# DLRM tower on one core: eight tables looked up by matmul in the first group, 260 gathers, gathered blocks taken four ahead, and half-block runs of Gram strips

## The reference, cut to what matters

```python
e = stack([tbl_f[ids[:, f]] for f in range(26)], axis=1)     # 2048 x 26 x 128
all_emb = concatenate([bottom[:, None, :], e], axis=1)       # 2048 x 27 x 128
gram = einsum('bfd,bgd->bfg', all_emb, all_emb)
z = gram[:, triu_i, triu_j]                                  # 351 pairs
h = concatenate([z, bottom], axis=1)                         # 479
h = maximum(h @ W_top1 + b_top1, 0)                          # 512
h = maximum(h @ W_top2 + b_top2, 0)                          # 256
y = h @ W_top3
```

## Time and profile before

| | us |
|---|---|
| median of 3 runs | 356.62 (356.36 to 359.17) |
| the profiled execution | 355.85 |
| its span, first to last instruction | 354.1 |
| PE busy | 329.4 (93%) |
| POOL busy (264 gathers) | 255.7 (72%) |
| DVE busy | 245.1 (69%) |
| ACT busy | 205.0 (58%) |
| granted PE clock | 1.0 throughout |

### The profile page before, as it was taken

The page is one execution under the profiler, slowest core; times in us unless marked ns, Lnnn a source line. Parts: engine busy times, 40 slices in busy tenths (PEclk is TensorE's granted clock), DMA queues, the critical chain, the costliest instruction groups (busy, mean ns, idle before and its releaser), DMA issues.

```text
span 354.1 us, 13649 instructions
## 1 busy us (share of the span) xinstructions
PE 329.4 (93%) x5840; PEld 295.9 (84%) x5840; DVE 245.1 (69%) x720; ACT 205.0 (58%) x349; POOL 255.7 (72%) x274
## 2 busy tenths in 40 slices
PE   0788989999999999999999989999999999999996
PEld 0676979998888989979888889879999798888885
DVE  1999989996676978459763987549885597431412
ACT  3684777522345659549478567565865587572222
POOL 5777777777777777777777777777777777777720
PEclk9999999999999999999999999999999999999999
DMA  6668649422228685576685496584769476532210
GB/s 206 189 173 219 184 127 316 121 55 54 55 54 159 95 165 114 83 155 136 148 115 98 98 175 123 121 99 99 158 125 141 99 130 113 115 83 56 56 31 1
DMA packets 64203, 42.88 MB, mean 121 GB/s; under 512 B 48784, under 2 KB 56464, under 8 KB 64016
## 3 DMA queue, kind: packets, MB, share of 16 engines
q1 hardware_dynamic: 55024, 24.38, 34.8%
q0 software_dynamic: 8448, 17.32, 20.8%
q10 hardware_dynamic: 672, 0.33, 0.3%
HBM read 31.24 MB, written 0.01 MB: 88 GB/s over the span
## 4 chain that ended last, share of the span: by engine, by line
PE 82%; DVE 9%; DMA 3%; ACT 2%; issue 2%; SPq 0%; ACTq 0%; DVEq 0%
PE hot_ps L498 30%; PE gram_ps L476 14%; PE h_ps L530 11%; PE xt_ps L498 9%; PE h_ps L575 8%; DVE onehot L731 5%; PE h_ps L527 4%; PE xt_ps L459 3%; DMA rows_sb<-in_rows_dram 2%; DVE tab L798 2%; PE zt_ps L512 2%; DMA ids_wide<-in_hot_ids_dram 1%; DVE h L788 1%; ACT turned L993 1%; DVE Z L739 1%
## 5 line engine op out<-in xcount | busy, mean ns | idle before, releaser
L445 POOL DMA_INDIRECT X<-in_table_dram,rows_sb x264 | 254.3, 963 | 82.8 <-issue 78.9
L731 DVE TENSOR_SCALAR onehot<-ids_wide,row_value 128x288 fp32r<-128x288 int16 (+2 forms) x575 | 183.9, 390 | 31.6 <-PE hot_ps L498 20.6
L498 PE MATMUL hot_ps<-onehot,tab 128*128 128x288 f32 (+2 forms) x948 | 144.6, 305 | 14.1 <-DVE onehot L731 13.8
L498 PEld LDWEIGHTS hot_ps<-onehot,tab 128*128 128x128 f32 x948 | 132.0, 190 | 17.7 <-issue 15.4
L706 ACT COPY XT<-turned 128x512 int16<-128x512 int16 x82 | 65.7, 885 | 8.7 <-DMA turned<-planes 8.7
L883 ACT COPY XT<-hot_ps 128x288 f32<-128x288 f32 (+2 forms) x66 | 40.1, 658 | 39.8 <-PE hot_ps L498 37.5
L476 PEld LDWEIGHTS gram_ps<-XT 128*27 128x27 f32 x4096 | 45.1, 104 | 20.9 <-issue 15.8
L476 PE MATMUL gram_ps<-XT 128*27 128x26 f32 x4096 | 56.3, 192 | 4.2 <-issue 1.2
L872 ACT COPY planes<-X 128x1024 int16<-128x1024 int16 x41 | 44.3, 1082 | 17.5 <-DMA X<-in_table_dram,rows_sb 17.5
L530 PE MATMUL h_ps<-stage_sb,w_sb 128*128 128x256 f32 (+3 forms) x192 | 44.2, 366 | 0.0
L530 PEld LDWEIGHTS h_ps<-stage_sb,w_sb 128*128 128x128 f32 (+1 forms) x192 | 35.0, 191 | 4.3
(11 more groups left out here) (54 smaller groups left out, 137.8 us busy)
## 6 DMA issues: line engine op xcount, KB each, us to landing
stage_sb<-in_hot_dram SPq DMA_DIRECT2D x20, 256.0 KB, 3.5
X<-in_table_dram,rows_sb POOLq DMA_INDIRECT x264
ids_wide<-in_hot_ids_dram SPq DMA_DIRECT2D x8, 360.0 KB, 5.3
ids_wide<-in_hot_ids_dram SPq DMA_DIRECT2D x4, 400.0 KB, 4.0
bottomT<-in_bottom_t_dram SPq DMA_DIRECT2D x8, 128.0 KB, 3.9
w_sb<-in_w_dram SPq DMA_DIRECT2D x1, 1024.0 KB, 7.0
turned<-planes SPq DMA_TRANSPOSE x41
stage_sb<-in_hot_dram SPq DMA_DIRECT2D x5, 128.0 KB, 2.9
```

The lines of the kernel that those rows point to most:

```text
L445: pool.indirect_dma_start(X[:, n % RING, k, :], None, table, bass.IndirectOffsetOnAxis(idx[:, column:column + 1], 0)).then_inc(gathered[n ...
L498: mm = pe.matmul(hot_bank(i)[:, 0:width(n)], tab[u][:, part, D * c:D * (c + 1)], onehot[p % ONEHOTS][:, c - BITES[u][h], 0:width(n)], star ...
L731: compared = dve.tensor_scalar(onehot[p % ONEHOTS][:, c - BITES[u][h], 0:width(n)], ids_wide[:, k, 0:width(n)], row_value[:, c:c + 1], Non ...
```

## The change

- Group 0 looks up 8 tables: 70 chunks, 140 products, all 256 wide. The four further tables of tiles 0 and 1 are now two, and are fetched for both tiles by one side unit of four gathers into Z, after units 0 and 1. Gathers: 264 to 260.
- The X ring has 5 slots instead of 4. ACT splits unit b+4 in its step b instead of b+2 (so 50 units go by DMA, 10 to 59, instead of 41). PE transposes unit b+4 at block b while that is below 10.
- PE works in pairs of blocks throughout. Strips come 16 to a run, each between lookups or layers; two quarters of layer 1, or both tiles of layer 2, stand together between the two runs of the pair's first block. `z_transposes` moves to a pair's end. Layer 2 writes the two tiles to two halves of its bank.
- The third bank for lookups is used from group 2 on, was 3. Ids are loaded three blocks before a group's end.
- In the head DVE clears gram_ps and adds the row offsets later, makes the one-hots of a piece before its subtraction, and the first piece is halved.
- `last_blocks` starts at block 56. Units 60 to 63 are transposed by PE inside the strips of blocks 58 to 60 and ahead of those of 62; layer 2 of tile 14 comes after the last strip.

PE at blocks 16 to 19 before: the last rows of a group 288 wide, the pair of 64 strips, z, and the next pair with layer 1 (hot_ps and xt_ps are lookup banks, gram_ps the strips).

```diff
-ALWAYS = 16
-SOMETIMES = 4
-HOT = TABLES - ALWAYS
-HOT_BASE = HOT - SOMETIMES
+GATHERED = 16
+EXTRA = 2
+HOT = TABLES - GATHERED
+HOT_BASE = HOT - EXTRA
 FOUR = 4
 BLOCKS = P // PAD
-TILE_COLUMNS = BLOCKS * (1 + ALWAYS // FOUR)
-BOTTOM_SLOT = ALWAYS + SOMETIMES
+TILE_COLUMNS = BLOCKS * GATHERED // FOUR
+BOTTOM_SLOT = GATHERED + EXTRA
-RING = 4
+RING = 5
 TURNED = 2
-AHEAD = 2
 SHARING = 2
...
-SPLIT_STEPS = 6
+SPLIT_STEPS = 3
...
-LAST = BLOCKS * (TILES - 2)
+UNITS = BLOCKS * TILES
+LAST = UNITS - 2 * BLOCKS
+THIRD = 2
-THIRD = 3
...
+LEAD = 4
+SIDE = UNITS
+STREAM = [0, 1, SIDE] + list(range(2, UNITS))
+HEAD_TURNS = {1: 0, 2: 1, 4: SIDE, 6: 2, 7: 3}
+TURN_FROM, TURN_TO = 10, UNITS - BLOCKS
+BY_DMA = list(range(TURN_FROM, TURN_TO))
+DIRECT = [n for n in STREAM if n not in BY_DMA]
 NTH = {n: k for order in (DIRECT, BY_DMA) for k, n in enumerate(order)}
+MOVED = {n: k + 1 for k, n in enumerate(STREAM)}
...
-    PIECE = [pieces(c, PIECE_MAX) for c in HC]
+    PIECE = [([0, 2] if u == 0 else [0]) + pieces(c, PIECE_MAX)[1:] for u, c in enumerate(HC)]
...
+                if b == STARTS[n + 1] - 3 and n + 2 < GROUPS:
+                    load_low_ids(n + 2)
+                if b == STARTS[n] and 0 < n < GROUPS - 1:
                     load_high_ids(n + 1)
+                if b + LEAD in BY_DMA:
+                    turn(b + LEAD)
...
+            for n in STREAM:
+                if n == BLOCKS:
                     pool.wait_ge(idx_ready, 1)
+                if n == SIDE:
+                    pool.wait_ge(side_ready, 1)
+                    for k in range(FOUR):
+                        pool.indirect_dma_start(side[:, k, :], None, table,
+                                                bass.IndirectOffsetOnAxis(side_sb[:, k:k + 1], 0)
+                                                ).then_inc(side_gathered, 16)
+                    continue
                 before = n - RING
                 if before >= 0 and before in BY_DMA:
                     pool.wait_ge(planes_ready, NTH[before] + 1)
                 elif before >= 0:
                     pool.wait_ge(xt_full, NTH[before] + 1)
...
+                dve.wait_ge(h2_full, t + 1 if t >= TILES - 2 else t + 2 - t % 2)
+                dve.tensor_tensor(h2[:], h2_half(t), vec_sb[:, 0, :], ALU.add).then_inc(h2_moved, 1)
...
+                    dve.wait_ge(side_loaded, 16)
+                    dve.tensor_tensor(side_sb[:, 0:FOUR], side_sb[:, 0:FOUR], side_sb[:, FOUR:2 * FOUR], ALU.add
+                                      ).then_inc(side_ready, 1)
+                    dve.wait_ge(rows_loaded, 16)
+                    dve.tensor_tensor(chunks[:, 1:, :], chunks[:, 1:, :],
+                                      starts.to_broadcast([P, TILES - 1, TILE_COLUMNS]), ALU.add).then_inc(idx_ready, 1)
                 for p in asked_of(q):
                     one_hot(p)
+                split_second(q)
+            dve.memset(gram_ps[:], 0.0).then_inc(pads_zero, 1)
...
-                split_words(UNITS_OF.get(b + AHEAD, []))
+                for i in placed_in(b):
+                    if i not in ended(b):
+                        place_hot(i)
                 for p in pieces_ended(b):
+                    if is_last(p) and ASKED[p][0] in placed_in(b):
+                        place_hot(ASKED[p][0])
                     one_hot_share(p + ONEHOTS)
-                for i in placed[1:]:
-                    place_hot(i)
+                split_words(b + LEAD)
                 if j == 2:
                     place_bottom(t + 1)
                 for q in LATE_PIECES[PER_STEP * b:PER_STEP * (b + 1)]:
                     split_first(q)
-                moves(b + 1)
+                if b + LEAD < TURN_FROM:
+                    move(b + LEAD)
+                if b + LEAD - 1 in BY_DMA:
+                    move(b + LEAD - 1)
...
+            def pair(b):
+
                 t, j = b // BLOCKS, b % BLOCKS
+                between = t >= 2 and (t % 2 == 1 or j == 2) and b + 2 < LAST
+                if between:
                     lookups(*slice_of(b))
+                    strips(b, 0, 1)
+                    layers(t, j)
+                    strips(b, 1, RUNS)
                 else:
                     for run in range(RUNS):
                         lookups(*slice_of(b, run, run + 1))
+                        strips(b, run, run + 1)
+                if b + LEAD < TURN_FROM:
+                    transposes(b + LEAD)
+                for run in range(RUNS):
+                    lookups(*slice_of(b + 1, run, run + 1))
+                    strips(b + 1, run, run + 1)
+                if not between:
+                    layers(t, j)
+                if j == 0 and t > 0:
+                    z_transposes(t - 1)
...
                 layer1(len(JOBS) - 2, 1)
-                gram(b + 1)
-                transposes(UNITS_OF[b + 2])
+                strips(b + 1)
                 layer1(len(JOBS) - 2, 2)
                 layer1(len(JOBS) - 2, 3)
-                gram(b + 2)
-                transposes(UNITS_OF[b + 3])
+                transposes(b + 3)
+                strips(b + 2)
+                strips(b + 3)
                 bottoms_last(0, C1 - 1)
-                gram(b + 3)
-                layer2(t - 1, 0, C1 - 1)
+                layer2(t - 1)
                 z_transpose_last(0)
```

More of the change, by code:

```diff
@@ L123, in folded_pairs, with build @@
     return out
[L126 removed]
+def build(nc, table, rows_in, side_in, hot_ids, hot_tables, bottom_t, w1, b1, w2, row_vecs, out):
     fp32, fp32r, i16, i32 = mybir.dt.float32, mybir.dt.float32r, mybir.dt.int16, mybir.dt.int32
@@ L462, in gram, with transposes @@
[L462 to L472 removed]
+            def transposes(n):
+                if n not in DIRECT:
+                    return
+                if n == SIDE:
+                    pe.wait_ge(side_gathered, 16 * FOUR)
+                else:
+                    pe.wait_ge(gathered[n % RING], 16 * FOUR * (n // RING + 1))
+                if NTH[n] > 0:
+                    pe.wait_ge(xt_moved, MOVED[DIRECT[NTH[n] - 1]])
+                for k in range(FOUR):
+                    rows = side[:, k, :] if n == SIDE else X[:, n % RING, k, :]
+                    mm = pe.transpose(xt_ps[:, P * k:P * (k + 1)], rows, ident[:])
+                mm.then_inc(xt_full, 1)
@@ L697, in move_turned, with move_direct @@
-        def move_turned(eng, copy, n):
-            t, j = UNITS[n]
-            slot = NTH[n] % TURNED
+                if u in HEAD_TURNS:
+                    transposes(HEAD_TURNS[u])
+            for b in range(0, LAST, 2):
+                pair(b)
+            last_blocks()
+        def move_direct(eng, copy, b):
+            eng.wait_ge(xt_full, NTH[b] + 1)
+            if b == SIDE:
+                copy(XT[:, 0:2 * BLOCKS, :, GATHERED:GATHERED + EXTRA],
+                     xt_ps[:].rearrange("d (k b s) -> d b s k", k=EXTRA, s=PAD)).then_inc(xt_moved, 1)
+                return
+            wait(eng, gram_full, b - KEPT + 1)
+            copy(XT[:, b % KEPT, :, 0:GATHERED].rearrange("d s (k f) -> d s k f", f=FOUR),
+                 xt_ps[:].rearrange("d (k s f) -> d s k f", s=PAD, f=FOUR)).then_inc(xt_moved, 1)
@@ L1073 @@
     out = nc.dram_tensor("out_0_dram", (P, TILES), _mybir.dt.float32, kind="ExternalOutput").ap()
-    build(nc, dram["table"], dram["rows"], dram["hot_ids"], [dram[f"hot{u}"] for u in range(HOT)],
+    build(nc, dram["table"], dram["rows"], dram["side"], dram["hot_ids"], [dram[f"hot{u}"] for u in range(HOT)],
           dram["bottom_t"], dram["w1"], dram["b1"], dram["w2"], dram["vecs"], out)
```

317 lines of the change are left out of this document (127 added, 190 removed).

## The result

The changed kernel takes 358.39 us (median of 20 runs, 357.24 to 361.89), the kernel before 356.95 on the same chips: a ratio of 1.0051, 95% interval 1.0028 to 1.0075. It is half a per cent slower, well within 1%. The forecast was 356.7, no change. The profiled execution has a span of 359.0 and took 360.73, which is 2.3 above its median: in six of the 20 runs, this one among them, the mean granted clock of TensorE is 0.995 or lower, and they take 359.4 to 361.2, while the other 14 have a median of 358.1.

A forecast was written before the change was run, and what follows sets the result against it. PE was taken as the bound, with POOL's gathers right behind. Terms of 6.6 - 2.7 - 2.9 - 2.1 + 2.0 - 1.4 + 0.6 summed to +0.1, giving 356.7 us by the median; range from just under 352.2 to 361.

The forecast's parts named there:

- Head: Before block 0: two more tables and the later gram_ps clear, less an earlier second table, add 6.6 us.
- Blocks 0 to 7: PE transposes six units instead of ten and block 4's double transposition goes: 2.7 us saved.
- the paragraph on the gathers: POOL's stream: four fewer gathers take 5.0 us off; a shift from late side-unit indices is priced at nothing.
- Blocks 8 to 15: Seven units are no longer transposed by PE: 2.9 us saved.
- Blocks 16 to 53: Sixteen strips a run, with restarts, layers and layer 2's waits, save 2.1 us; new Z waits add 2.0.
- The restart: In blocks 16 to 53, each of 43 more runs of lookups costs 0.18 us: +7.7.
- The waits for Z: PE's first strips of five even tiles (4 to 12) wait for DVE's Z: +2.0 us in all.
- The end: Last blocks and tail: units of blocks 57 to 59 leave PE, -1.4 us; later layer work adds 0.6.
- POOL's last gather: The last gather of the stream was forecast to start near 333.4 us.
- Rival 2: DVE falls behind in pairs starting an even tile, PE waits longer for Z: +5.5 us, 362.2; 12%.
- Rival 3: In the head, DVE starts the second table no sooner: +2.3 us, 359.0, no change; 10%.
- Rival 1: Restarts cost nothing or Z is never waited for; gathers bind at the last unit: -4.4 us, 352.2; 21%.

The follow-up runs named there:

- the run with one block less ahead: The changed kernel with the units PE transposes itself (4 to 9) turned three blocks ahead instead of four: 357.99 us, ratio 1.0026 to the kernel before.
- the run with 20 lookups: The changed kernel with the first block of each even tile and of tile 1 as 20 lookups, then 32 strips: 355.17 us, ratio 0.9944 to the kernel before.

## Why the prediction was right, and where it was not

It was right in the number that counts, +0.1 forecast and +1.4 measured in the medians, and in most terms. In part that was luck: a head that came 1 to 1.5 cheaper than forecast paid for some of the waits that the forecast had at nothing.

- **Head, +6.6 forecast, +6.1 measured.** PE waits 1.34 for unit 3 at its end, but block 0 could not have begun at once without that wait: it needs its one-hots too, and where PE hardly waits for unit 3 it begins at 36.59 and 37.06, which is +5.1 and +5.6. The term that was too large is the table of ten chunks. It costs DVE 3.9 (the last subtractions of the three that there are now start at 26.66, 30.56 and 34.46), not the 4.4 read from the last table before, and three times 0.5 is 1.5. The second table did start 2.3 sooner, as forecast: its first piece is begun with one-hots at 10.39 now and was begun with a subtraction at 12.69.

```profile
10.39 0.88 DVE L739 TENSOR_SCALAR onehot<-ids_wide,row_value 128x256 fp32r<-128x256 int16 x3
11.19 0.73 DVE L806 TENSOR_TENSOR tab<-stage_sb,tab 128x512 fp32r<-128x512 f32 x1
```

- **Blocks 0 to 7, -2.7 forecast, +1.9 measured.** Less 3.0 of waits and 1.45 of slow clock it is -2.5. In the two other profiles of this part it is -0.2 and -0.9, or -2.8 and -2.4 less their waits of 2.6 and 1.5. The term was sound; what failed is the paragraph on the gathers: "it has up to 5 us to spare, so I price this at nothing." The 5 us were read at the last unit, and so were the 2.9 from a gather's start to its use. Early, PE takes about 4.5 us a block and POOL 5.0 a unit, the lead of four asks for a unit earlier, and units 3, 4 and 6 were in use only 5.9, 5.0 and 6.1 after their last gather's start (31.24, 37.65 and 48.11). Four gathers fewer give 1.2. The sentence "I am wrong altogether if PE waits for XT, that is for the units four blocks ahead" named the place. The waits came, before the transpositions out of X that fill XT, and cost about a microsecond of the median rather than the forecast.
- **Blocks 8 to 15, -2.9 and -2.4**: 0.26 is a wait for Z in tile 2.
- **Blocks 16 to 53, -0.1 and -0.5.** The restart is there. In the timeline of PE of the changed kernel 18 lookups in one run last 2.54 to the next strips, nine 1.38, so a second run costs 0.22 (0.19 against the 18 that stand behind strips, 181.43 to 184.00), where 0.18 stood:

```profile
171.06 2.62 PE L516 MATMUL xt_ps<-onehot,tab 128*128 128x288 f32 x18
173.60 0.42 PE L494 MATMUL gram_ps<-XT 128*27 128x26 f32 x32
...
179.70 1.46 PE L516 MATMUL hot_ps<-onehot,tab 128*128 128x288 f32 x9
181.08 0.42 PE L494 MATMUL gram_ps<-XT 128*27 128x26 f32 x32
```

  The waits for Z in tiles 4, 6, 8, 10 and 12 are 0.56, 0.24, 0.66, 0.20 and 0.25, together 1.9 where 2.0 stood. That strips and restarts cancel could not be shown by undoing one of them, since either kernel loses 13 to 16 us without the parts around it; only the sum is shown.
- **The end, -0.8 and -0.2.** Two small waits for ScalarE and DVE, 0.56 and 0.49, took what was missing.
- **POOL's last gather** came at 336.66, 3.3 late, of which the two gathers of 2.22 in the head make 2.6. The forecast itself was sound: 333.8 to 334.2 in three of the experiments.

Rival 2 did not happen: no Z wait passes 0.7. Rival 3 did not happen either, though the time lies near its 359.0: the second table came when forecast. Rival 1 (gathers bind, faster) had the right engine and the wrong place: they hold PE up early, and once the Z waits are gone they take back in the first half what PE wins. Its other half, that a restart might cost nothing, falls with the 0.22 above: here the trace does not bear out what the Trainium skill (TensorE: Matmul & The Clock Gate, Architectural detail) would allow, loads pulled forward over the strips.

## What to carry to other kernels

Two streams that end together need not run together: read the slack of the slower one at several points of the timeline, not at the last transfer, and look for it in the waits of the engine between them (here ScalarE), since the bound engine's own waits show nothing until the slack is gone. Before a profile is explained, look at a second one of the same program: here the early part alone differed by 3 us. The lead of units, the length of a run and the orders of the helping engines are one choice: one of them changed alone lost 10 to 16 us in three trials. And six waits of 0.2 to 0.7, one line of the page, were the cheapest to repair: 3.2 us for three lines of code.

## What the runs showed of the hardware that I had not expected

A short pause of PE can be followed by a lower granted clock that costs over half as much again: after 2.52 us, and after 2.19 in the run with one block less ahead, some 1.45 us were lost on slow matmuls. After 1.89 in the run with 20 lookups the granted clock was 0.70 for 5.8 us. The length of the pause does not decide it alone: 1.77 us before unit 4, with the weights held back, left the clock at full, and so did 2.82 before unit 6 with the gathers doubled:

```profile
57.25 0.66 PE L475 MATMUL xt_ps<-ident,X 128*128 128x128 f32 x4 [2.82 <-DMA X<-in_table_dram,rows_sb]
57.66 1.70 PE L522 MATMUL hot_ps<-onehot,tab 128*128 128x288 f32 x11
```

The pause of 2.19 us within a run of strips was ended by no semaphore. It fell 7 to 9 us behind the issue of the weights (45.5 to 46.4), but eight other profiles with the weights in place at that time have no such pause. The profiler's instruction queue moved a packet between 53.0 and 53.5 in that run, at the start of the pause, and none from 45 up to there. That PE's own instructions were late is possible, and not shown.
